# Routed layers of a macaron block on one Trainium2 core: three of sixteen router-weight comparisons moved from VectorE to GpSimd

## What is computed

```python
x = x + 0.5 * _L0_ffn_ref(_layernorm(x), ...)      # routed, stage ffn_a
x = x + _L0_attn_ref(_layernorm(x), ...)           # latent attention
x = x + 0.5 * _L0_ffn_ref(_layernorm(x), ...)      # routed, stage ffn_b
x = x + 0.5 * _L1_ffn_ref(_layernorm(x), ...)      # stage mix_a
x = x + _L1_attn_ref(_layernorm(x), ...)           # attention
x = x + 0.5 * _L1_ffn_ref(_layernorm(x), ...)      # stage mix_b
```

```python
K = int(CAPACITY * S)                              # 0.125 * 512 = 64
weights = jnp.einsum('bsd,do->bso', x, W_r).squeeze(-1) + b_r
topk_vals, topk_idx = jax.lax.top_k(weights, K)
threshold = topk_vals[:, -1]
sel_mask = weights > threshold[:, None]
xg = jnp.take_along_axis(x, topk_idx[..., None], axis=1)
h = jax.nn.gelu(jnp.einsum('bkd,df->bkf', xg, W1) + b1)
blk = jnp.einsum('bkf,fd->bkd', h, W2) + b2
gate = (topk_vals > threshold[:, None])
vals = blk * (wg * gate)[..., None]                # wg: the weights of the picked
processed = jnp.zeros_like(x).at[bidx, topk_idx].add(vals)
return processed + x * (~sel_mask)[..., None]
```

## Time and profile before

| | |
|---|---|
| median of three runs | 1937.31 us (1936.6 to 1941.16) |
| the profiled execution | 1940.07 us, of which the span of the core is 1938.3 us |
| mean granted TensorE clock | 0.932 of full speed |
| stage ffn_a, start of its statistics to the next stage's | 5.8 to 85.7 us |
| stage ffn_b, likewise | 1218.8 to 1296.0 us |
| comparisons in ffn_a (L334) | 33.04 to 52.27 us |
| comparisons in ffn_b (L334) | 1244.31 to 1263.53 us |

### The profile page before, as it was taken

One profiled execution on the slowest core, in us unless ns is written; L12 is line 12 of the kernel. 1 busy time (PEld: TensorE's weight loads), 2 busy tenths in 40 slices (PEclk: granted clock), 3 DMA queues, 4 the chain that ended last, 5 costly groups with the idle time before them and its releaser, 6 DMA issues. The chain is left out here.

```text
span 1938.3 us, 27188 instructions
## 1 busy us (share of the span) xinstructions
PE 1717.4 (89%) x9368; PEld 1003.3 (52%) x9368; DVE 1531.0 (79%) x2236; ACT 1181.3 (61%) x2043; POOL 983.2 (51%) x820
## 2 busy tenths in 40 slices
PE   4667999999999999999999998565979899999986
PEld 3554555556565555565565654455644344444445
DVE  6772888998997988988889887677566988888816
ACT  1045787777776777778777776111325377778760
POOL 0004799897896997988979988002412000000110
PEclk8776999999999999999999999677987699999998
DMA  3100000000000000000000000111330200110001
GB/s 101 55 24 24 1 1 1 15 1 12 3 1 15 1 1 15 1 15 1 1 7 1 1 1 1 47 47 38 76 77 2 34 1 2 21 15 2 2 1 44
DMA packets 26697, 34.34 MB, mean 18 GB/s; under 512 B 5312, under 2 KB 19648, under 8 KB 26432
## 3 DMA queue, kind: packets, MB, share of 16 engines
q1 hardware_dynamic: 25360, 31.28, 6.8%
q10 hardware_dynamic: 1200, 1.31, 0.2%
HBM read 26.03 MB, written 6.29 MB: 17 GB/s over the span
## 5 line engine op out<-in xcount | busy, mean ns | idle before, releaser
L1208 POOL TENSOR_TENSOR lath_summed<-lath_summed,lath_held 128x512 f32<-128x512 f32 x392 | 524.0, 1337 | 54.4 <-ACT lath_held L1114 27.5
L1925 ACT ACTIVATE atth_probs<-atth_score 128x512 f32<-128x512 f32 (+3 forms) x640 | 293.2, 539 | 141.4 <-PE atth_score L1844 139.8
L1279 DVE TENSOR_TENSOR lath_held<-lath_held,lath_shift 128x1024 f32<-128x1024 f32 (+2 forms) x352 | 331.5, 970 | 24.6 <-PE lath_shift L1027 15.1
L1108 ACT ACTIVATE lath_held<-lath_score 128x1024 f32<-128x1024 f32 (+2 forms) x352 | 283.6, 828 | 105.5 <-DVE lath_largest L1232 52.1
L1114 ACT ACTIVATE lath_held<-lath_held 128x1024 f32<-128x1024 f32 (+2 forms) x352 | 292.6, 861 | 50.3 <-DVE lath_held L1279 48.6
L1884 DVE TENSOR_REDUCE atth_maxima<-atth_slot 128x2 f32<-128x1024 f32 (+3 forms) x288 | 287.3, 1043 | 42.1 <-PE atth_slot L1827 41.1
L1014 PE MATMUL lath_out<-lath_held,lat_latent 128*64 128x512 f32 (+1 forms) x1152 | 303.0, 591 | 7.9 <-ACT lath_held L1114 4.3
L998 PE MATMUL lath_score<-lath_query_hi,lat_key_hi 128*128 128x512 f32 x576 | 246.8, 428 | 22.4 <-ACT lath_held L1108 17.2
L1772 POOL TENSOR_SCALAR_AFFINE_SELECT atth_probs<-atth_probs 128x512 f32<-128x512 f32 x64 | 40.6, 635 | 419.1 <-ACT atth_probs L1925 419.1
L1003 PE MATMUL lath_score<-lath_query_hi,lat_key_lo 128*128 128x512 f32 x576 | 231.2, 401 | 0.0
L1232 DVE TENSOR_TENSOR lath_largest<-lath_score,lath_largest 128x1024 f32<-128x1024 f32 (+2 forms) x240 | 211.7, 882 | 17.5 <-PE lath_score L1003 12.5
(11 more groups left out here) (345 smaller groups left out, 2894.6 us busy)
## 6 DMA issues: line engine op xcount, KB each, us to landing
att_first_query<-att_scratch SPq DMA_DIRECT2D x12, 256.0 KB, 8.9
atth_query<-att_scratch SPq DMA_DIRECT2D x12, 256.0 KB, 9.7
ffn_a_w<-in_L_ffn_W SPq DMA_DIRECT2D x2, 1024.0 KB
lat_raw_out<-in_L_attn_w_out SPq DMA_DIRECT2D x8, 256.0 KB, 2.7
lat_rope<-in_c_rope_feature SPq DMA_DIRECT2D x1, 2048.0 KB, 10.7
ffn_b_w<-in_L_ffn_W SPq DMA_DIRECT2D x2, 1024.0 KB, 7.1
mix_a_factors<-in_L_ffn_factors SPq DMA_DIRECT2D x8, 256.0 KB, 4.2
att_scratch<-attp_high SPq DMA_DIRECT2D x4, 512.0 KB, 2.8
```

Source lines behind the costliest of these rows:

```text
L1108: nc.scalar.activation(part_columns(slot(n), tiles, q0), part_columns(score_bank[n % 2], tiles, q0), ACT.Copy)\
L1208: nc.gpsimd.tensor_tensor(total, total, slot(n)[:, i, :], ALU.add).then_inc(s["tiles_summed"], 1)
L1279: nc.vector.tensor_tensor(columns, columns, added, ALU.subtract)\
L1925: nc.scalar.activation(probs[:, step % PROB_STEPS, h, q0:CH], score_bank[u % 3][:, q0:CH], ACT.Exp, scale=SCALE1)\
```

## The change

In both routed layers the comparisons of tiles 4, 9 and 14 are done by GpSimd, into a ring of two buffers of its own, `not_above_pool`. VectorE does the other thirteen in its ring of three, its `counted` waits now set by its own list of tiles. TensorE keeps the order t = 0 to 15 and takes each tile from the ring in which it is, waiting on `compared` or on the new `compared_pool`. GpSimd waits for all four chunks of the row and for the new `weight_kept`, raised by the last copy of `weight`, on which VectorE now waits in place of the `link`; before its third comparison it waits until its first has been counted.

```diff
--- before.py
+++ after.py
@@ -24,6 +24,8 @@
 DFF = 1024
 NF = DFF // P
 KEPT_BEFORE = 14
+POOL_TILES = (4, 9, 14)
+VECTOR_TILES = tuple(t for t in range(NT) if t not in POOL_TILES)
 SCATTER_BANKS = (0, 4, 1, 5)
 CAPACITY = 64
 
@@ -284,6 +286,7 @@
         weight_row = sb("weight_row", [P, TOKENS])
         weight = sb("weight", [P, NT])
         not_above = sb("not_above", [P, 3, TOKENS], BF16)
+        not_above_pool = sb("not_above_pool", [P, 2, TOKENS], BF16)
         chosen, keep_scale, take_scale = sb("chosen", [P, NT]), sb("keep_scale", [P, NT]), sb("take_scale", [P, NT])
         ranks = sb("ranks", [P, 3, NT])
         onehot, onehot_t = sb("onehot", [P, NT, P]), sb("onehot_t", [P, NT, P])
@@ -295,7 +298,7 @@
         loading = Loading(core, ctx) if first else None
         norm = Norm(core, ctx, tag, xn, xn_t, bank, loading)
         names = ("weights_loaded ffn_loaded wide_ready weight_bank row_ready weight_turned compared counted chosen_ready"
-                 " prefix_done onehot_ready picked_done picked_t_ready hidden_done"
+                 " prefix_done onehot_ready picked_done picked_t_ready hidden_done weight_kept compared_pool"
                  " hidden_ready block_done block_ready onehot_turned onehot_t_act onehot_t_dve scattered added").split()
         s = {n: core.sem(f"{tag}_{n}") for n in names}
 
@@ -313,6 +316,16 @@
                              allow_slow_non_contiguous=True).then_inc(s["ffn_loaded"], 16)
                 sp.dma_start(b2[:], inp["L0_ffn_b2"].partition_broadcast(P)).then_inc(s["ffn_loaded"], 16)
 
+            @block.gpsimd
+            def _(pool):
+                pool.wait_ge(s["row_ready"], NCH)
+                pool.wait_ge(s["weight_kept"], 1)
+                for k, t in enumerate(POOL_TILES):
+                    if k >= 2:
+                        pool.wait_ge(s["counted"], POOL_TILES[k - 2] + 1)
+                    nc.gpsimd.tensor_scalar(not_above_pool[:, k % 2], weight_row[:], weight[:, t:t + 1], None,
+                                            ALU.is_le).then_inc(s["compared_pool"], 1)
+
             @block.vector
             def _(dve):
                 link = Link(core, dve, f"{tag}_dve_link")
@@ -327,11 +340,12 @@
                     dve.wait_ge(s["weight_turned"], c + 1)
                     w = nc.vector.tensor_copy(weight[:, TPC * c:TPC * (c + 1)],
                                               bank[4 + c][:].rearrange("p (t q) -> p t q", q=P)[:, :, 0])
-                link(w)
-                for t in range(NT):
-                    if t >= 3:
-                        dve.wait_ge(s["counted"], t - 2)
-                    nc.vector.tensor_scalar(not_above[:, t % 3], weight_row[:], weight[:, t:t + 1], None,
+                w.then_inc(s["weight_kept"], 1)
+                dve.wait_ge(s["weight_kept"], 1)
+                for k, t in enumerate(VECTOR_TILES):
+                    if k >= 3:
+                        dve.wait_ge(s["counted"], VECTOR_TILES[k - 3] + 1)
+                    nc.vector.tensor_scalar(not_above[:, k % 3], weight_row[:], weight[:, t:t + 1], None,
                                             ALU.is_le).then_inc(s["compared"], 1)
                 dve.wait_ge(s["counted"], NT)
 
@@ -424,9 +438,16 @@
 
 
                 for t in range(NT):
-                    pe.wait_ge(s["compared"], t + 1)
+                    if t in POOL_TILES:
+                        k = POOL_TILES.index(t)
+                        pe.wait_ge(s["compared_pool"], k + 1)
+                        smaller = not_above_pool[:, k % 2]
+                    else:
+                        k = VECTOR_TILES.index(t)
+                        pe.wait_ge(s["compared"], k + 1)
+                        smaller = not_above[:, k % 3]
                     for i in range(NT):
-                        last = nc.tensor.matmul(bank[0][:, i:i + 1], not_above[:, t % 3, i * P:(i + 1) * P], core.ones_b[:, 0:1],
+                        last = nc.tensor.matmul(bank[0][:, i:i + 1], smaller[:, i * P:(i + 1) * P], core.ones_b[:, 0:1],
                                                 start=(t == 0 and i == 0), stop=(t == NT - 1 and i == NT - 1))
                     last.then_inc(s["counted"], 1)
                 pe.wait_ge(s["chosen_ready"], 1)
```

## The result

The changed kernel takes 1960.57 us (median of four runs, 1959.47 to 1971.87) against 1936.95 us for the kernel before. The ratio is 1.0131, with a 95% interval of 1.0108 to 1.0153, or 21 to 30 us: it is slower by 23.6 us by the medians. That is the sign forecast and more than three times the size: 6.9 us were forecast, and the end of the range was 1956.

A forecast was written before the change was run, and what follows sets the result against it. VectorE's comparisons were taken to bound both routed layers. Per layer, GpSimd's three take 7.05 us out of VectorE and the three removed return 3.59: +6.9 us in two layers, 1937.3 + 6.9 = 1944.2 us, range 1937 to 1956.

The forecast's parts named there:

- What bounds the stretch: Comparison stretch of both routed layers: VectorE is the chain, and a comparison taken off it is worth up to 1.20 us.
- Exclusion: VectorE's comparisons beside GpSimd's: each GpSimd instruction takes its own length, less 0.19 us, out of VectorE.
- The length D: Duration of one GpSimd comparison of 128x2048, absent from the trace: taken as 2.54 us from the one-input AFFINE_SELECT.
- the prediction's own sum: Both routed layers: six GpSimd comparisons change the time by 6 x (D - 0.19 - 1.20), forecast as +6.9 us.
- The upper bound of D: Longest length allowed for one GpSimd comparison: 4.41 us, from the slope of the two-input TENSOR_TENSOR.
- The order and its limit: TensorE's counts at t = 4, 9, 14: never wait for GpSimd while its comparison lasts below about 4.8 us.
- Small edits at nothing: weight_kept for the link, 8 KB more SBUF per partition, GpSimd joining the block and barrier: no cost.
- The clock: TensorE at 0.50 in the comparison stretch; its later rise moves the gather up to 1.4 us per layer, +/-3 us both.
- (D): Rival: VectorE and GpSimd don't shut each other out, so the kernel is 7.2 us faster, 1930.1 us; chance 0.07.
- (C): Rival: in turn, GpSimd's comparison cheap at 1.75 to 2.2 us, +2.2 to +4.9 us, about 1940.5; chance 0.22.
- (B): Rival: in turn, GpSimd's comparison dear at 3.2 to 4.4 us, +11 to +18 us; chance 0.26.
- (E): Rival: GpSimd's first comparison of a layer late by several us, VectorE and TensorE stand; about 1949 us; chance 0.04.

The follow-up runs named there:

- experiment 5: Kernel before, all sixteen comparisons on VectorE, with three GpSimd copies of the row per layer that nobody reads: 1948.31 us, ratio 1.0052.
- Experiment 2: Kernel before plus a list of GpSimd instructions in ffn_a, varying operation, types and size, for whose end VectorE waits: 2063.45 us, one run.
- Experiment 4: Changed kernel with only one comparison per layer on GpSimd (tile 9) and fifteen on VectorE: 1951.21 us, ratio 1.0053.
- experiment 3: VectorE's comparisons also write an accumulator: in the changed kernel 1962.92 us, ratio 1.014; in the kernel before, all sixteen on VectorE, 1974.24 us, one run.
- experiment 6: Changed kernel with GpSimd's three comparisons per layer replaced by copies of a row of zeros: 1944.49 us, ratio 1.0027.

## Why the prediction was wrong

- **What bounds the stretch: right.** VectorE was the chain and a comparison is worth 1.20 us there. What the stretches gained reached the ends of their stages, but for the 0.7 us of the gather and small change: 22.5 of 23.7 us.
- **Exclusion: right, shown.** "I take L334 to be shut out in the same way" as L248: six comparisons were lengthened, three per layer, the other twenty untouched, as the prediction asked for. The price is a GpSimd instruction's length less 0.25 to 0.3 us (5.44 gives 5.19 at most and 15.45 / 3 = 5.15 on average in the changed kernel, 1.89 gives 1.63 in experiment 5); 0.19 was read from the earlier trace rows.
- **The length D: the step that failed.** "I take 2.54, from the row nearest in kind." It is 5.44 us. With it the prediction's own sum, with its own overlap, is 6 x (5.44 - 0.19 - 1.20) = 24.3 us, and with 0.25 it is 23.9; 23.6 were measured. The mechanism was right and one term was put at less than half of its size. Why GpSimd's TENSOR_SCALAR is so long is not shown, only that its operation and types don't make it so.
- **The upper bound of D: wrong as well, and worse.** The 4.41 us were meant as an end. It rested on the thought that two inputs must cost more than one. Experiment 2 shows one-input TENSOR_SCALAR at 2.54 ns an element and the two-input addition at 1.67. Number of inputs doesn't rank GpSimd's operations. "Nearest in kind" was not near either: AFFINE_SELECT, with the fixed part that the prediction took off, has the slope of the copy (0.82 against 0.83 ns), and TENSOR_SCALAR three times that. The 1.03 or 2.03 cycles of the Trainium skill's page "GPSIMD Engine Reference", section "Performance pitfalls for Q7 kernels", 1.76 or 3.46 us by the estimate beside the sum, were too low as well: 2.54 ns are 3.0 cycles at that page's 1.2 GHz.
- **The order and its limit.** "TensorE never waits for GpSimd while D is below about four of VectorE's periods, 4.8 us." D was above, and TensorE still never waited for it (the view of waits names VectorE alone). The limit was put in us where it had to be put in turns: while GpSimd works VectorE stands, so the deadline moves with it. GpSimd's third comparison ended at 49.91 + 7.64 = 57.55 and was counted at 63.91, 6.4 us later. The detail of turns was off: the third came in after seven of VectorE's had passed, not after five: two of them passed while it waited, and its 7.64 us hold 2.2 of waiting.
- **Small edits at nothing: right.** Experiment 4 finds a third of the loss for a third of the work (3.98 of 11.85 us of stretch), so nothing is left for weight_kept, GpSimd's joining or the barrier.
- **The clock: right in size.** The gather changed by -0.7 us in ffn_a and by under 0.1 in ffn_b, within the 1.4 allowed. In ffn_a the granted clock was still 0.50 from 60 to 62 us before, 3 to 5 us into the gather, and 0.81 from 73 to 75 in the changed kernel, 4 to 6 us into it. That the comparison stretch runs at 0.50 was not quite so: it begins at 1.00 and falls to 0.50 within 4 us in both versions, hence the means of 0.57 in the earlier trace rows and 0.54 here.
- **The rivals.** (D), no exclusion, is refuted for this form and holds for the accumulator form (experiment 3). The line rate of one-input work that it names fits the copy, 0.83 ns an element, and not TENSOR_SCALAR, 2.54 ns. (C) is what experiment 6 measured with a copy of 1.89 us: +1.30 us per layer by the stretch. (B) was the nearest and still ended at 4.4. (E), a late first comparison, did not occur; two MODIFY_POOL_CONFIG are there for this operation, at 0.8 us, long before, and ffn_a's comparisons are no longer than ffn_b's. "The ordinary operations have none" was a misreading: in the trace of before the TENSOR_TENSOR of L1214 has two as well, at 144.0 us.

## What to carry to other kernels

Before work is moved to an idle engine, ask whether that engine and the one relieved can run at the same time in the very forms used: a pair of rows in which one of them is lengthened by the other's duration (here L248 in mix_a) is a strong sign for the same operation, and experiment 3 shows that another form of it can behave otherwise. If they can't, the move pays only if the new engine's instruction, less the small overlap, is shorter than the old one's. A duration that the trace lacks may not be bounded by operations with more inputs; price the operation family by itself. And look at all idle engines: ScalarE needs 1.6 times VectorE's time per comparison but doesn't hold it up, and gave 15 us where GpSimd cost 24.

## What was not expected of the hardware

GpSimd's TENSOR_SCALAR costs 5.37 to 5.44 us for 128x2048 with each operation and type tried, 2.9 times the copy with the same conversion (1.89 us) and 1.5 times a two-input addition (3.60 us). And VectorE's comparison is held by GpSimd only in its fast form, the one without accumulator: 1.28 us become 6.47, while the accumulator form, 2.34 us, stays at 2.34 beside the same GpSimd instructions.
